# Three PSUM banks each for scores and turned probabilities, and an exponential ahead of a copy, in a kernel of two cross attentions

## The reference

```python
normed = x * rsqrt(mean(x**2) + 1e-6) * norm_w
q, k, v = heads(normed @ wq), heads(ctx @ wk), heads(ctx @ wv)   # 16 heads of 64
x1 = x + concat_heads(softmax(q @ k.T) @ v) @ wo                 # no scaling of the scores
out = x1 + softmax(x1 @ ctx.T) @ ctx
```

## Time and profile before

| what | value |
|---|---|
| median of 3 runs | 693.33 us (693.3 to 693.69) |
| the profiled execution | 693.43 us |
| its span, first to last instruction | 691.7 us |
| TensorE matmul busy | 673.7 us (97%) |
| ScalarE busy, VectorE busy | 468.1 us (68%), 465.6 us (67%) |
| granted TensorE clock | 1.0 |

### The profile page before, as it was taken

How to read it: one execution, slowest core, us unless ns; L and a number is a source line. 1 busy time by engine, 2 the same in 40 slices (tenths; PEclk the granted TensorE clock), 3 DMA queues, 4 the chain that set the end, 5 groups by cost and what they waited for, 6 DMA issues and landing times.

```text
span 691.7 us, 13320 instructions
## 1 busy us (share of the span) xinstructions
PE 673.7 (97%) x4764; PEld 611.9 (88%) x4764; DVE 465.6 (67%) x994; ACT 468.1 (68%) x1168; POOL 161.5 (23%) x485
## 2 busy tenths in 40 slices
PE   5999999999999999999999999999999999999997
PEld 4788989998999889999899988999899988999896
DVE  3576765777667775677756776677756777576744
ACT  4776676677666766677666776667766677666753
POOL 2221124111331214221141213311133121412120
PEclk9999999999999999999999999999999999999999
DMA  5022112211122111312012110211012120211100
GB/s 190 1 54 16 9 12 54 15 10 9 15 54 16 9 8 18 59 9 16 2 23 53 15 10 15 53 16 9 8 15 54 16 13 4 21 10 9 16 12 7
DMA packets 25566, 16.50 MB, mean 24 GB/s; under 512 B 14334, under 2 KB 23838, under 8 KB 25502
## 3 DMA queue, kind: packets, MB, share of 16 engines
q1 hardware_dynamic: 25502, 15.66, 16.2%
HBM read 15.19 MB, written 0.46 MB: 23 GB/s over the span
## 4 chain that ended last, share of the span: by engine, by line
PE 90%; ACT 5%; DVE 2%; issue 1%; DMA 1%; POOL 0%; POOLq 0%; ACTq 0%
PE ps_o L969 28%; PE ps_t L945 19%; PE ps_s L917 10%; PE ps_s L921 10%; PE ps_s L918 10%; PE ps_m L991 4%; PE ps_m L866 3%; ACT probs L555 3%; PE ps_o L982 2%; PE ps_t L879 2%; PE ps_o L984 1%; DMA x_rows<-in_x_dram 1%; DVE part_max L699 1%; PE ps_m L1038 1%; ACT pT L546 1%
## 5 line engine op out<-in xcount | busy, mean ns | idle before, releaser
L546 ACT ACTIVATE pT<-ps_t 128x496 fp32r<-128x496 f32 (+1 forms) x312 | 182.7, 588 | 179.4 <-PE ps_t L945 177.2
L699 DVE TENSOR_REDUCE part_max<-ps_s 124x1 f32<-124x512 f32 (+2 forms) x336 | 209.4, 651 | 58.6 <-PE ps_s L921 57.5
L969 PE MATMUL ps_o<-pT,c_both 128*128 128x248 f32 (+2 forms) x1632 | 242.8, 291 | 0.6 <-DVE result L750 0.5
L685 DVE TENSOR_TENSOR pT<-ps_t,pT 128x496 fp32r<-128x496 f32 (+3 forms) x312 | 192.0, 623 | 69.6 <-ACT pT L546 67.8
L969 PEld LDWEIGHTS ps_o<-pT,c_both 128*128 128x128 f32 x1632 | 219.4, 189 | 3.7 <-DVE pT L685 2.6
L555 ACT ACTIVATE probs<-ps_s,neg_max 124x512 f32<-124x512 f32 (+2 forms) x336 | 219.4, 664 | 4.1 <-DVE neg_max L704 4.1
L945 PE MATMUL ps_t<-ident,probs 124*128 124x124 f32 (+2 forms) x1232 | 183.9, 267 | 3.9 <-DVE pT L685 1.9
L945 PEld LDWEIGHTS ps_t<-ident,probs 124*128 124x128 f32 (+2 forms) x1232 | 145.9, 140 | 43.9 <-ACT probs L555 10.3
L429 POOL CAST tails<-probs 124x36 fp32r<-124x36 f32 (+2 forms) x224 | 40.9, 215 | 489.1 <-ACT probs L555 489.1
L917 PE MATMUL ps_s<-cT_hi,q_hi 128*124 128x512 f32 (+3 forms) x312 | 143.4, 460 | 0.9 <-DVE q_lo L685 0.9
L921 PE MATMUL ps_s<-cT_hi,q_lo 128*124 128x512 f32 (+3 forms) x312 | 118.8, 381 | 0.0
(11 more groups left out here) (130 smaller groups left out, 488.7 us busy)
## 6 DMA issues: line engine op xcount, KB each, us to landing
ctx_raw<-in_ctx_dram SPq DMA_DIRECT2D x8, 704.0 KB
rinv_row<-denominator_rows SPq DMA_DIRECT2D x39, 124.0 KB, 3.7
rinv_row<-denominator_rows SPq DMA_DIRECT2D x8, 186.0 KB, 3.5
denominator_rows<-rinv SPq DMA_DIRECT2D x39, 1.0 KB
wq_sb<-in_L_xattn_wq_dram SPq DMA_DIRECT2D x2, 256.0 KB, 5.5
wk_sb<-in_L_xattn_wk_dram SPq DMA_DIRECT2D x2, 256.0 KB, 5.7
wv_sb<-in_L_xattn_wv_dram SPq DMA_DIRECT2D x1, 512.0 KB, 7.3
wo_sb<-in_L_xattn_wo_dram SPq DMA_DIRECT2D x1, 512.0 KB, 8.3
```

What stands on the lines that cost most here:

```text
L546: act.activation(dst, ps_t[:, turn_bank("item", g, c), 0:nj * m] .rearrange("p (j m) -> p j m", m=m), ACT.Copy).then_inc(turned_hi, 1)
L685: dve.tensor_tensor(dst, src, hi.bitcast(F32), ALU.subtract).then_inc(done, 1)
L699: mx = dve.tensor_reduce(part_max[0:m, k, c:c + 1], ps_s[0:m, score_bank(g, c), 0:CHUNKS[c][1]], AX.X, ALU.max)
L969: t = pe.matmul(ps_o[:, 0, 0:w], weights, moving, start=(i == 0), stop=(i == UNITS - 1))
```

## The change

The banks of `ps_s` go from four to three, and each chunk number has its own. Chunk `c` of item `g` waits for exponential `c` of item `g - 1`. The bank goes to `ps_t`, which has three; a turn waits for the lo of the turn three back. The rest follows from the banks: the first context's third part is turned into `ps_t` bank 2 instead of `ps_s` bank 3, a wait for a start-up copy moves from turn 1 to turn 2 of item 0, and near the end the spread of the denominators waits for an exponential of its bank. In ScalarE's order, exponential 0 of item `g` moves ahead of hi copy 2 of `prev`.

```diff
     def turn_bank(what, at, c):
-        return (TURNS.index((what, at, c)) + 1) % 2
+        return (TURNS.index((what, at, c)) + 1) % 3
 
     def score_bank(g, c):
-        return (NC * g + c) % 4
+        return c
...
-        ps_s = ps("ps_s", 4)
-        ps_t = ps("ps_t", 2)
+        ps_s = ps("ps_s", NC)
+        ps_t = ps("ps_t", 3)
...
-        CTX0_BANKS = [ps_t[:, 0], ps_t[:, 1], ps_s[:, 3]]
+        CTX0_BANKS = [ps_t[:, 0], ps_t[:, 1], ps_t[:, 2]]
...
                     if prev is not None:
-                        for c in range(NC):
+
+                        for c in range(NC - 1 if here else NC):
                             turned_chunk_hi(prev, c)
...
                     if here:
                         for c in range(NC):
                             exp_chunk(g, c)
+                            if c == 0 and prev is not None:
+                                turned_chunk_hi(prev, NC - 1)
                             if c == 1 and pair is not None:
                                 pair_hi(pair[1], pair[0], ps_m[:, 0])
...
-                if NC * g + c >= 4:
-                    pe.wait_ge(exped, NC * g + c - 3)
+                if g > 0:
+                    pe.wait_ge(exped, ev(g - 1, c))
...
             def wait_turn_bank(what, at, c):
-                k = TURNS.index((what, at, c)) - 2
+                k = TURNS.index((what, at, c)) - 3
...
-                if g == 0 and c == 1:
+                if g == 0 and c == 2:
                     pe.wait_ge(wqk_ready, 4)
...
             pe.wait_ge(diag_made, 2)
+            pe.wait_ge(exped, ev(L_FIRST, 0))
```

## The result

| | before | after |
|---|---|---|
| median, run side by side | 693.32 us (692.75 to 693.69) | 698.17 us (696.83 to 698.4) |
| ratio | 1 | 1.0067, 95% interval 1.0054 to 1.008 |
| the profiled execution | 693.43 us | 696.83 us |
| its span | 691.7 us | 695.1 us |

The changed kernel is slower by 4.85 us; 2.6 were forecast. The median of after lies 1.3 us above its own profiled execution, so the comparison of the two traces has 3.4 us of span to explain (695.1 against 691.7), and the rest has a paragraph of its own. In the changed kernel the lines behind the exponentials' loop stand three lower: L917 is now L920, L945 is L948, L704 is L707, L612 is L615, L685 is L688; L546 and L555 stay.

A forecast was written before the change was run, and what follows sets the result against it. TensorE's own work was taken to set the time, with work in 97% of the span. Terms 1.2 + 0.3 + 0.15 + 0.33 + 0.65 = 2.6 us on 693.33 gave 695.9 us, own range 694.7 to 697.5.

The forecast's parts named there:

- The price that was not in the trace: Scores waiting for an exponential: 0.05 us from signal to scores taken; over some five places -0.3 to +0.7 us.
- the wide one: Range of the whole kernel's time for 8 in 10: 694.0 to 698.6 us.
- slower by more: Rival, batches 1 to 6: the 0.48 reaches PV in step 13 in full, 3.5 us more, 699.4 us; chance 0.12.
- The start: Batch 0, steps without PV: scores wait for exponential 0, item 4's scores start later; 1.2 us taken.
- Rest of batch 0: Batch 0, step 13: scores start at 93.13, exponential 0 signals at 93.46; 0.3 us lost.
- the even batches: Batches 2, 4, 6, steps 7 to 9: scores 0.3 and 0.6 later, then it comes back; 0.05 left each, 0.15 together.
- batch 7: Batch 7, step 13: the scores (0.70 us) wait for exponential 0, and only then the turn; 0.65 us later.
- the forecast's own rule: At each place: new signal of exponential 0 (negative maximum, 0.02, 0.77) + 0.05, against the start of the scores.
- The odd batches: Batches 1, 3, 5: scores wait a little, nearly paid back; in step 13 exponential 2 comes 0.11 later, 0.33 in all.

The follow-up runs named there:

- the repeat: The changed kernel run again with no edit: 698.18 us, ratio 1.0069.
- each half alone: Changed banks with ScalarE's old order: 708.71 us; the kernel before, with its four and two banks, with ScalarE's new order alone: 698.94 us.

## Why the prediction was right, and where it was off

**The mechanism.** Right: exponential 0 starts 0.04 us after the negative maximum in ordinary steps and gives the scores there 1.03 us, the scores wait for it at the start and in short steps, and the turns' waits for banks vanish. The price that was not in the trace, taken as 0.05 us from signal to scores, is 0.06 by three pairs of rows.

**The size.** The change was forecast at 2.6 us and measured 4.85, nearly twice as much. 698.17 us lies above the forecast's own range (694.7 to 697.5) and in the upper end of the wide one (up to 698.6), and the rival "slower by more", at 699.4, is nearer to it than the forecast. Between item 1 and the end of the sum, where starts and clock don't mix in, the traces have 3.99 and 4.21 us. That the total fell within the wide range is in part luck: that range was widened upward for a rival, not for the waits that made the difference.

**The start.** 1.2 forecast, 1.15 measured. The third turn bank gives nothing there, as said: three and two turn banks give 1.15 and 1.16. The old order there takes 0.49 off.

**Rest of batch 0, the even batches, batch 7.** 0.3, 0.05 each and 0.65 forecast; 0.31, 0.09 to 0.10 and 0.76 measured. (For step 13 of batch 0 the forecast's own rule gives 93.46 + 0.05 - 93.13 = 0.38, not 0.3.) Within batch 2 the scores of steps 8 and 9 start 0.24 and 0.59 later by the traces, where 0.3 and 0.6 were forecast. That even batches shift and get it back is borne out from the other side: without the third turn bank they lose 0.46. In batch 7, step 13, the forecast took 0.70 us for the chunk's scores, and they take 0.79 to the start of the turn behind them:

```profile
660.26 0.48 PE L920 MATMUL ps_s<-cT_hi,q_hi 128*112 128x512 f32 x1 [1.59 <-ACT probs L555]
...
661.05 0.59 PE L948 MATMUL ps_t<-ident,probs 124*128 124x124 f32 x4
```

**The odd batches: the term that was mis-sized.** The forecast had 0.11 each. They took 0.47, 0.52 and 0.50, together 1.16 more than forecast, out of the 1.39 by which the table's sum exceeds 2.6. The step that failed is: "With the copy 0.66 later there (0.18 in step 9 and 0.48 in step 10) the scores at 333.55 wait a little, which the bank waits of 0.15 and 0.09 nearly pay back". Two things stand in its place. The copy of step 9 is late by 0.49, not 0.18, because the late item's hi copy (157.93) now stands between exponential 0 and it like any other; with step 10's it is 0.94. And the scores are held at three places: chunk 0's for exponential 0 twice (164.76 and 171.27, worth 0.17 and 0.29) and chunk 2's for exponential 2 (167.38, worth 0.37). The forecast had looked at exponential 0 alone, although the banks tie every chunk's scores to the exponential of its own chunk. The freed bank waits are larger than forecast too: 0.34 a batch stay when the loss is taken out, and 0.77 is what the third bank is worth in all. My own mark ("wrong if batches 1 to 6 change by more than 0.3 us each") was passed by the odd batches. The rival in which late copies of odd batches don't fit was right about the place for them, not about the even ones and not in sending the loss to PV in step 13 in full.

**The rest of the median.** The forecast for the profiled execution was 693.43 + 2.6 = 696.0 us, and it took 696.83. The median is 698.17. Of the 1.3 between, the repeat shows two sources of the spread: the start ahead of item 1, 25.33 to 27.16 us in the executions profiled here, and TensorE's clock at the end, worth about 2 us when it falls early. The forecast had neither. The clock shows best in the version with the old order in steps 9 and 10: three executions at a mean clock of 1.0 took 693.73 to 694.21 us, six at 0.997 or less 695.76 to 696.47. Its median is one of the slower kind, so its distance to other medians is less sure than the table. Whether the change makes the fall of the clock more frequent isn't settled: 5 of 9 executions of the changed kernel have a mean of 0.998 or less, as have 10 of the 29 executions of the kernel before that the last versions were compared with. Compared like with like, the fall isn't what separates the two kernels: set against those 29, it is 4.5 us slower among the executions at 0.999 and 1.0 (medians) and 4.3 among the others.

**Not tried:** four banks for scores together with three for turns, as with `ps_o` and `ps_m` that makes nine banks, one more than there are here.

## What to carry to other kernels

A bank given from one ring to another turns a wait of the one into a wait of the other: write down for each chunk which signal its bank now waits for, and compare it with the need in the shortest step, not in the ordinary one. Here each half alone cost more than both (14.9 and 6.0 us against 4.0, by the table's sums), because the order brings exponentials early for scores and lo copies late for turns, and the third turn bank pays for the second. A copy moved into a loop is paid once for each pass that stands before the next free wait, so go through all steps that follow each other on that engine and through every chunk, the one-off items among them; and where a new order helps only in some steps, use it in those alone.

## What the runs showed of the hardware

TensorE's granted clock can fall at the very end of an execution, and in two executions of the same program it did so differently: 1.0 to the last instruction in one profile, 0.50 from 688.7 us in another, after waits such as this one in the second:

```profile
688.26 0.48 PE L948 MATMUL ps_t<-ident,probs 100*128 100x100 f32 x3 [0.68 <-ACT probs L555]
```

The other profile has the same wait of 0.68 us there and kept its clock, so the wait alone doesn't decide. The cost was about 2.1 us of 698. Where it falls later it costs less: with three banks for scores and two for turns the clock fell at 693.4 of 699.9 us and the end took 1.6 us longer; with the old order in steps 9 and 10 it fell at 692.3 of 693.4, behind the last matmul, and the end took its usual 28.79. And the start up to item 1 differed by up to 1.8 us between profiled executions that are alike ahead of it; a difference under 2 us between two single executions is read from stages, not from the totals.
